# A one-core hybrid block: bias and first powers ahead of the constants, later moments inside sequence 0, and three of four block rows copied by ScalarE

## What is computed

```python
x = x + attention(layernorm(x))      # 16 heads of 16, rotary, causal softmax
x = x + routed_spline(layernorm(x))  # own layer norm, 64 routes, min and max of each route over all tokens
x = x + gated_delta(layernorm(x))    # 16 heads of 128: convolutions, silu, scan over time, norm, gate, projection
x = x + routed_spline(layernorm(x))
```

```python
err = einsum('bhvk,bhk->bhv', S, kt) - vt
S = at * S - bt * err * kt
o = einsum('bhvk,bhk->bhv', S, qt)
```

## Time and profile before

| what | value |
|---|---|
| median of 3 runs | 3283.73 us (3281.1 to 3285.6) |
| profiled execution | 3282.32 us, span on the core 3280.5 us |
| PE busy | 2930.4 us, 89% |
| DVE busy | 2502.4 us, 76% |
| ACT busy | 2093.4 us, 64% |
| POOL busy | 1810.0 us, 55% |
| granted TensorE clock, mean | 0.951 |

### The profile page before, as it was taken

One profiled execution on the slowest core, in us unless ns is written; L12 is line 12 of the kernel. 1 busy time (PEld: TensorE's weight loads), 2 busy tenths in 40 slices (PEclk: granted clock), 3 DMA queues, 4 the chain that ended last, 5 costly groups with the idle time before them and its releaser, 6 DMA issues.

```text
span 3280.5 us, 60794 instructions
## 1 busy us (share of the span) xinstructions
PE 2930.4 (89%) x19888; PEld 2424.4 (74%) x19888; DVE 2502.4 (76%) x6374; ACT 2093.4 (64%) x4556; POOL 1810.0 (55%) x1914
## 2 busy tenths in 40 slices
PE   5999999945769999999999999999999999977763
PEld 3777777734558888888888888888888888865652
DVE  4556666575658888888887887888888888889986
ACT  2556555523547777777777777777777777755531
POOL 1111111142677668676676767768676686766442
PEclk9999999957889999999999999999999999989985
DMA  2000000002566656656666566565666566543311
GB/s 94 1 0 0 0 0 0 1 28 87 160 189 193 187 173 172 203 161 191 189 173 198 151 201 200 157 196 173 189 188 178 175 179 194 165 128 92 103 34 52
DMA packets 572121, 422.74 MB, mean 129 GB/s; under 512 B 228691, under 2 KB 475219, under 8 KB 571734
## 3 DMA queue, kind: packets, MB, share of 16 engines
q1 hardware_dynamic: 571862, 419.51, 43.9%
HBM read 276.39 MB, written 143.01 MB: 128 GB/s over the span
## 4 chain that ended last, share of the span: by engine, by line
PE 73%; DVE 12%; POOL 7%; issue 3%; ACT 3%; DMA 1%; SPq 0%; POOLq 0%; DVEq 0%; ACTq 0%
PE bank L1999 25%; PE bank L2050 15%; PE bank L2147 6%; PE bank L1853 5%; POOL oT L812 4%; PE bank L2055 3%; PE bank L1828 3%; PE bank L1765 3%; PE bank L1838 3%; PE bank L2030 2%; PE bank L2038 1%; ACT oT L1099 1%; DVE acc L1546 1%; PE bank L1807 1%; PE bank L1823 1%
## 5 line engine op out<-in xcount | busy, mean ns | idle before, releaser
L779 POOL TENSOR_TENSOR acc<-acc,shifted 128x510 f32<-128x510 f32 x384 | 585.5, 1527 | 550.1 <-DVE acc L1546 546.9
L1546 DVE SCALAR_TENSOR_TENSOR acc<-bank,conv_w,acc 128x254 f32<-128x254 f32 (+1 forms) x1536 | 628.8, 471 | 98.8 <-ACT acc L1029 95.4
L1999 PE MATMUL bank<-x_k,w_kq 128*128 128x256 f32 x2048 | 504.0, 391 | 13.6 <-DMA x_k<-xT_scratch 9.4
L1027 ACT ACTIVATE shifted<-bank,conv_w 128x255 f32<-128x255 f32 x768 | 366.9, 478 | 218.5 <-issue 147.4
L1029 ACT ACTIVATE acc<-bank,conv_b,conv_w 128x256 f32<-128x256 f32 x768 | 439.8, 573 | 0.0
L1999 PEld LDWEIGHTS bank<-x_k,w_kq 128*128 128x128 f32 x2048 | 378.8, 194 | 81.3 <-issue 31.9
L796 POOL TENSOR_TENSOR inv<-inv,outer 128x30 f32<-128x30 f32 (+14 forms) x480 | 259.5, 541 | 37.6
L2147 PE MATMUL bank<-w_o,oT 128*128 128x256 f32 x1024 | 246.5, 385 | 33.4 <-POOL oT L812 33.4
L793 POOL TENSOR_TENSOR outer<-inv 128x30 f32<-128x30 f32 (+14 forms) x480 | 235.3, 490 | 30.3 <-DMA inv<-L_scratch 2.5
L2030 PE MATMUL bank<-kq 128*128 128x256 f32 x1024 | 244.4, 382 | 5.1 <-ACT kq L1039 4.0
L2147 PEld LDWEIGHTS bank<-w_o,oT 128*128 128x128 f32 x1024 | 190.7, 191 | 77.8 <-issue 52.1
(11 more groups left out here) (237 smaller groups left out, 6544.4 us busy)
## 6 DMA issues: line engine op xcount, KB each, us to landing
abc<-decay_scratch SPq DMA_DIRECT2D x64, 512.0 KB, 5.9
q_scratch<-kq SPq DMA_DIRECT2D x64, 512.0 KB, 6.8
L_scratch<-LM SPq DMA_DIRECT2D x64, 512.0 KB, 3.4
M_scratch<-LM SPq DMA_DIRECT2D x64, 512.0 KB, 6.6
LTm<-L_scratch SPq DMA_DIRECT2D x64, 512.0 KB, 4.5
MTm<-M_scratch SPq DMA_DIRECT2D x128, 256.0 KB, 4.3
kqm<-q_scratch SPq DMA_DIRECT2D x64, 512.0 KB, 4.3
k_scratch<-knw SPq DMA_DIRECT2D x64, 258.0 KB, 4.8
```

The lines of the kernel that those rows point to most:

```text
L779: pool.tensor_tensor(dst, dst, shifted[:, u % 2, :, 1:], ALU.add).then_inc(Z["sumk" if u < 4 else "sumv"], 1)
L1027: act.activation(shifted[:, u % 2, i % 2, 1:], pj[:, 0:SEQ - 1], ACT.Copy, scale=conv_w[:, kind, bass.ds(head, 1), TAPS - 2:TAPS - 1].rear ...
L1546: dve.scalar_tensor_tensor(out=acc[:, kind, i, t:], in0=pj[:, 0:SEQ - t], scalar=wcol, in1=acc[:, kind, i, t:], op0=ALU.mult, op1=ALU.add) ...
L1999: mm = pe.matmul(dst[:, i * SEQ:(i + 1) * SEQ], w[:, k, head * DK:(head + 1) * DK], x[:, k, :], start=(k == 0), stop=(k == CT - 1))
```

## The change

Four things are edited in the preparation, one in the sweeps. POOL adds to the 21 semaphores of `A` alone at first, splits the bias next, then does the constants up to the masks, the first eight powers, the other constants, and then the additions to the 124 semaphores of `R` and `Z`. PE starts after 7 counts of `consts` and waits for `loaded_a` behind `tokens(0)`; ACT starts after the first count with a copy of one column of `ident`, and waits for all 13 behind its first copy. DVE waits for all 13 constants behind the normalisation of sequence 0. `moments_of(1)`, `(2)` and `(3)` move into `examined` parts 0, 1 and 3 of sequence 0, and the wait for the 24 other powers moves from between minima 1 and 2 to the end of that body; the moments use a semaphore of their own. In slots 64 to 73 of the gated-delta layer DVE copies one of the four block rows and ACT three. The diff, without new names and counters of semaphores:

```diff
-            for signals in (A, R, Z):
-                for signal in signals.values():
-                    pool.sem_inc(signal, 1)
+            for signal in A.values():
+                pool.sem_inc(signal, 1)
             ch = Chain(pool, p_step)
+            pool.wait_ge(loaded_bias, 32)
+            ch.link(pool.tensor_copy(bias_part[:, 0], bias[:]))
+            ch.link(pool.tensor_tensor(bias_rest[:], bias[:], bias_part[:, 0], ALU.subtract))
+            ch.link(pool.tensor_copy(bias_part[:, 1], bias_rest[:]))
+            ch.link(pool.tensor_tensor(bias_rest[:], bias_rest[:], bias_part[:, 1], ALU.subtract))
+            pool.tensor_copy(bias_part[:, 2], bias_rest[:]).then_inc(split_bias, 1)
...
+            pool.wait_ge(A["var"], past(1))
+            pool.wait_ge(consts, 3)
+            pool.tensor_tensor(rstd[:, 0:8], rstd[:, 0:8], half_neg[:, 0:8], ALU.pow).then_inc(A["rstd"], 1)
             pool.memset(rot[:], 0.0).then_inc(consts, 1)
...
+            for signals in (R, Z):
+                for signal in signals.values():
+                    pool.sem_inc(signal, 1)
...
         @block.scalar
-            act.wait_ge(consts, 13)
+            act.wait_ge(consts, 1)
+            act.copy(warm[:], ident[:, 0:1])
...
-                tokens(0), values_in(0), turned_in(0, 0), turned_in(0, 1)
+                tokens(0)
+                act.wait_ge(consts, 13)
+                values_in(0), turned_in(0, 0), turned_in(0, 1)
...
-                    for i in range(HG // 2, HG):
+                    for i in range(HG // 2 if s < STEPS else 1, HG):
                         ins = act.copy(vn[hp][q:q + BLK, 0, i], bank[3][i * BLK:(i + 1) * BLK, 0:DK])
...
-                    for i in range(HG // 2, HG):
+                    for i in range(HG // 2 if s < STEPS else 1, HG):
                         ins = act.copy(r1[q:q + BLK, i], bank[5][i * BLK:(i + 1) * BLK, 0:DK])
...
         @block.vector
-            dve.wait_ge(consts, 13)
...
                 def examined(part):
                     if first(b):
+                        if part == 0:
+                            dve.wait_ge(loaded_rest, 48)
+                            moments_of(1)
+                        if part == 1:
+                            moments_of(2)
                         if part == 2:
                             slope_signs()
+                        if part == 3:
+                            moments_of(3)
+                            dve.tensor_scalar(rstd[:, 8:], moments[:, 8:, 1], EPS, None, ALU.add).then_inc(A["var"], 1)
                         return
...
-                if first(b):
-                    dve.wait_ge(A["rstd"], past(2))
                 minima(2), minima(3)
...
                 weighted_values(1)
+                if first(b):
+                    dve.wait_ge(A["rstd"], past(2))
 
             normalised(0)
-            dve.wait_ge(loaded_rest, 48)
-            moments_of(1, 3)
+            dve.wait_ge(consts, 13)
             dve.wait_ge(loaded_a, 80)
...
                 rope(0, 0, ch), rope(0, 1, ch)
-                moments_of(2, 8)
-                moments_of(3, 11)
-                dve.tensor_scalar(rstd[:, 8:], moments[:, 8:, 1], EPS, None, ALU.add).then_inc(A["var"], 1)
...
-                    for i in range(HG // 2):
+                    for i in range(HG // 2 if s < STEPS else 1):
                         ins = dve.tensor_copy(vn[hp][q:q + BLK, 0, i], bank[3][i * BLK:(i + 1) * BLK, 0:DK])
...
-                    for i in range(HG // 2):
+                    for i in range(HG // 2 if s < STEPS else 1):
                         ins = dve.tensor_copy(r1[q:q + BLK, i], bank[5][i * BLK:(i + 1) * BLK, 0:DK])
...
         @block.tensor
-            pe.wait_ge(loaded_a, 80)
-            pe.wait_ge(consts, 13)
+            pe.wait_ge(consts, 7)
...
-                tokens(0), queries_keys(0, 0), queries_keys(0, 1), values_in(0), rotated(0, 0), rotated(0, 1)
+                tokens(0)
+                pe.wait_ge(loaded_a, 80)
+                queries_keys(0, 0), queries_keys(0, 1), values_in(0), rotated(0, 0), rotated(0, 1)
```

More of the change, by code:

```diff
@@ L176, in program @@
         stats = sb("stats", [P, 8, 6])
+        warm = sb("warm", [P, 1])
         gam = sb("gam", [P, C])
@@ L208, in program @@
         p_step = sem("p_step")
-        a_step = sem("a_step")
+        m_step = sem("m_step")
         stage_done = sem("stage_done")
@@ L1194, in _, with moments_of @@
             base = 0
-            def moments_of(t, count):
-                c = Chain(dve, v_step, count)
+            def moments_of(t):
+                c = Chain(dve, m_step, 3 * t)
                 for i in range(8):
@@ L1208, in _ @@
             dve.wait_ge(loaded_x, 16)
-            moments_of(0, 0)
+            moments_of(0)
             dve.tensor_scalar(rstd[:, 0:8], moments[:, 0:8, 1], EPS, None, ALU.add).then_inc(A["var"], 1)
             dve.wait_ge(A["rstd"], past(1))
-            dve.wait_ge(consts, 13)
-            base_a = 3 * (TILES // 8)
+            base_a = 0
             PER_A = 4
@@ L1373, in body @@
                 weighted_values(1)
+                if first(b):
+                    dve.wait_ge(A["rstd"], past(2))
             normalised(0)
-            dve.wait_ge(loaded_rest, 48)
-            moments_of(1, 3)
+            dve.wait_ge(consts, 13)
             dve.wait_ge(loaded_a, 80)
-            ch = Chain(dve, v_step, 6)
+            ch = Chain(dve, v_step, 0)
             def start():
                 rope(0, 0, ch), rope(0, 1, ch)
-                moments_of(2, 8)
-                moments_of(3, 11)
-                dve.tensor_scalar(rstd[:, 8:], moments[:, 8:, 1], EPS, None, ALU.add).then_inc(A["var"], 1)
             sequences(dve, start, body)
```

## The result

The changed kernel takes 3260.64 us (median of 4 runs, 3258.5 to 3264.13), the kernel before on the same chip 3284.66 us (4 runs, 3281.1 to 3289.51): a ratio of 0.9929, 95% interval 0.9914 to 0.9945. It is faster by 24.0 us (0.7%); the forecast was 30.9. The profiled execution took 3262.74 us, its span is 3260.9 us, and it is 19.6 us under the one of before (3282.32).

What follows compares the result with a forecast made beforehand. The prediction took a chain of waits to bound the first 80 us and DVE's own work the last 380. Gains of 18.8 and 12.1 us, 30.9 off the 3283.7 median, gave 3252.8 us, range 3247 to 3263.

Steps and rivals of the forecast that it cites:

- POOL, split, reload, power: Start: POOL free at 2.5 us, bias split to about 4.1, reload landed by 11 to 13, first power at 11.1.
- Rival (d): Start: first projection still waits for the reload, queued longer than thought; landing at 23 us gives 3261 us; chance 0.05.
- Normalisation, 0.73 us: Start: DVE normalises sequence 0 in 0.73 us behind the first power, done at 13.5 us.
- Table load, 1.3 us: Start: ACT's 1.28 us table load runs in DVE's shadow, so its copy follows the transposes at once.
- Moments in sequence 0, tokens of sequence 1 at 48.8 us: Sequence 0: with moments between minima, PE begins tokens of sequence 1 at 48.8 against 67.63 us, a gain of 18.8.
- Rival (a): Sequence 0: moments dearer than DVE's order says, costing 3.6 to 8 us, 3256 to 3261 us; chance 0.13.
- "No pause in my layout exceeds 2.2 us": Start: argument against a lasting half clock, PE's pauses staying within 2.2 us and over by 49 us.
- rival (c): Sequences 0 and 1: PE's half clock holds from the start, 0.77 us more per us of work; slower kernel; chance 0.03.
- Third moments, long power, last minima: Sequence 0's end: third moments and last minima lie beside PE's work to 54.7 us; nobody waits for the 4.18 us power.
- The tail, 12.1 us: Slots 64 to 73: moving 57 copies off DVE gains 12.1 us, 10.8 of it in slots 66 to 71.
- "just hidden": Tail sweeps: ACT's three copies, PE's row and gaps need 1.4 us against DVE's 1.5, priced at nothing.
- rival (b): Tail: ACT ends the sweeps and the 10.8 us vanish; 3264 us, 3279 by the lower bound; chance 0.11.

Runs made afterwards that it cites:

- e1: Changed kernel with the old two-to-two split of block rows in all sweeps, so only the preparation edits: 3262.5 us, 0.9916 of the kernel before.
- e2: Kernel before with only the new one-to-three split of block rows from slot 64 on: 3282.9 us, 0.9978 of the kernel before.
- e5: Changed kernel with POOL's clearing of `rot`, `q_scale` and `vx` moved ahead of its wait for the first variances: 3256.6 us, one run.
- e5b: Changed kernel with POOL held, before it clears `rot`, until the normalised rows are written: 3254.8 us, one run.
- e7: Changed kernel without ACT's early copy of one column of `ident`: 3265.7 us, one run.
- e3b: Changed kernel with unread transposes in both PE pauses of sequence 0, seven at 42.6 us and eight before the tokens of sequence 1: 3259.3 us.
- e8: Changed kernel with early `rot` clearing, late slope signs, seven unread transposes in PE's first pause and the old split in slots 65 and 73: 3253.7 us.
- e9: Changed kernel with the tail's sign product moved ahead of DVE's convolution in slots 64 to 73: 3260.2 us.
- e4: Changed kernel with the slope signs of sequence 0 moved from before the attention output to behind minima 11: 3261.5 us.
- e3: Changed kernel with eight unread transposes in PE's second pause, ahead of the tokens of sequence 1: 3259.1 us.

## Why the prediction was right, and where it was off

The forecast was 3252.8 us with a range of 3247 to 3263, the result 3260.6: the direction and the range held, the gain was a quarter smaller than the sum. Luck had a part in how close it came. In the profiled pair the edited stretches gave 17.1 us, little more than half of the sum; that the medians gave 24.0, and 27.4 and 6.9 for e1 and e2 alone in another session, shows how far they move. By its steps:

- **POOL, split, reload, power.** Right: 2.8, 4.0, reload issued at 10.72 and landed before PE asked for it at 17.05, power at 11.14. Rival (d) did not occur.
- **Normalisation, 0.73 us.** Wrong term: 2.22. The row it came from the earlier trace rows is from a time when POOL is idle; the prediction itself had `rot` follow the power at once, and did not ask what the two do to each other. Price 1.5 us at the first transposes, shown by e5 and e5b. It was hidden in the forecast by a second error of the other sign: the projections take 8.7 us there instead of 9.66, so the scores came at 27.6, 0.6 late.
- **Table load, 1.3 us.** Right: e7 gives 1.25.
- **Moments in sequence 0, tokens of sequence 1 at 48.8 us.** Right at 49.15, and DVE's order was as laid out. Rival (a), dearer moments, did not occur as such.
- **"No pause in my layout exceeds 2.2 us".** Nearly right in size (1.36 and 2.38; the layout's own 46.5 to 48.8 is 2.3 already) and wrong in what followed from it. The prediction took 18.8 us at the tokens and carried it unchanged to the start of sequence 1; rival (c) had a price for each us at the half level, but counted only on one that holds from the start on, and nothing between that and none. The clock fell behind such pauses and 5.8 us were lost. e3b and e8, where the first is filled and the second shortened or gone, and the clock stays up, speak for the pauses as the cause, with one profiled execution each. Nor did a busy PE regain its clock soon: it was busy without a gap for 12 us at the half level here and for nearly 20 in e2.
- **Third moments, long power, last minima.** Hidden, as forecast: DVE is idle for 6.8 us ahead of the first rotary step of sequence 1.
- **The tail, 12.1 us.** The term that missed most: 4.4 us. In slots 66 to 71, 36 copies of 0.30 us did leave DVE (10.8), but the slots shrank by 5.7. Of the 5.1 missing, 2.9 went to the sign product, for which the copies had been the cover against POOL's addition; 1.2 to DVE's new waits for PE's rows; about 1 to small lengthenings, such as the product with `ors` (1.52 us, 1.40 in e1). I read the waits as the longer turn of ACT that the prediction had called "just hidden", so rival (b) in small; but DVE also comes to each row 0.3 us sooner, and no run separates the two. The step that failed goes from "DVE hardly waits at all" to "each copy there is on the path": that is true of work that is taken away where nothing else comes up, and e9 shows how close the next thing was. Slot 64 gave 0.8 as forecast (0.9), but that is luck: it takes 34.3 us here and 35.1 to 35.3 in e3b, e4 and e7, as long as before (35.1). Slot 65 lost 0.5 (nothing forecast), and slots 72 and 73 together lost 0.9 (0.4 of gain forecast), with ACT's third copy last; in the other executions of the same code slot 72 lies anywhere from 26.2 to 27.7 us (26.96 before), so only the sign of slot 73 is sure.

In the profiled pair the sum is 12.7 + 2.5 + 4.4 = 19.6 us instead of 30.9; the medians gave 24.0. Where the difference lies, the executions without a trace do not say; their mean granted clock goes with their time (in the session of e1 the kernel before took 3278.9 to 3281.5 us at 0.951 to 0.952 and 3288.7 to 3293.2 at 0.946 to 0.947). The start of the kernel before is one place for it: e2 has the same start, and in its trace PE's pause at 48 us was 4.2 us long instead of 3.2, the half level held from 51.5 to 72 us instead of 53 to 56.5, and sequence 1 began at 92.4 us instead of 85.4.

```profile
56.00:72.00 16.00, 15.47 (x131) 0.99 0.01 1
```
```profile
56.00:72.00 16.00, 16.00 (x73) 0.50 0.00 0
```

(The stretch in the kernel before, then in e2.) The forecast stood on the execution with the shorter of the two starts.

## What to carry to other kernels

When an engine without waits is relieved of small instructions, ask what ran beside them on an engine that shares its way to SBUF, not only who waits for them: the copies here were the cover of somebody else's addition. A gain counts at the next point where the kernel is as busy as before, not at the point where the chain was cut; between the two, look at each new pause of TensorE and the granted clock behind it. And measure a small edit by distances between marks in the trace, which repeated to about 1 us over six slots where whole executions scatter by 3 to 17; take a second execution before believing less.

## What the runs showed of the hardware

- A normalisation on DVE (two of 128x256, fp32, SBUF to SBUF) took 2.22 us beside a POOL memset of 1.80 us that had started 0.09 us before it, and 0.73 without; bn_stats beside the same memset took its usual 2.71.
- A DVE product of two SBUF operands took 1.76 us against 1.20 when it started 0.68 us before the end of a POOL addition; a reduction in the same place was not held, and POOL's power took 2.00 instead of 1.01 beside the product.
- The clock fell behind a pause of 1.36 us (e3, e4), stayed low for 7 to 17 us with PE busy most of the time (20 us in e2), and did not fall where the pause was cut to 0.45 us, though one of 1.50 us followed 4 us later (e3b).
- At the very start the same projections take 3.41 + 1.98 us in the changed kernel and 3.78 + 2.84 in e3b, though the granted clock is given as 1.00 in both: 1.2 us of scatter that the column of the clock does not show. The four transposes ahead of them take 1.09 us in both, as they do at the half level at 49.15 us, so a 1.00 in that column is not to be relied on there.
